# Eight products for V, Q and K in four of fifteen groups, and a new order on ScalarE and GpSimd

## The reference

```python
q = relu(h @ Wq + bq); k = relu(h @ Wk + bk); v = relu(h @ Wv + bv)   # h = layernorm(x)
e = q @ k.T / sqrt(512), causal: e - 10000 above the diagonal
y = softmax(e) @ v
x1 = x + layernorm(relu(y @ Wo + bo))
x2 = x1 + layernorm(ffn(layernorm(x1)))
```

## Time and profile before

| | us |
|---|---|
| median of 2 runs | 2149.94 (2148.06 to 2151.82) |
| the profiled execution | 2151.1 |
| its span, first to last instruction | 2149.3 |
| TensorE busy in the span | 1989.5 |
| VectorE | 1674.9 |
| ScalarE | 1146.2 |
| GpSimd | 1258.6 |

### The profile page before, as it was taken

How to read it: one execution, slowest core, us unless ns; L and a number is a source line. 1 busy time by engine, 2 the same in 40 slices (tenths; PEclk the granted TensorE clock), 3 DMA queues, 4 the chain that set the end, 5 groups by cost and what they waited for, 6 DMA issues and landing times. The chain is left out here.

```text
span 2149.3 us, 35197 instructions
## 1 busy us (share of the span) xinstructions
PE 1989.5 (93%) x11039; PEld 1103.9 (51%) x11039; DVE 1674.9 (78%) x3468; ACT 1146.2 (53%) x2496; POOL 1258.6 (59%) x1421
## 2 busy tenths in 40 slices
PE   7889999978999998899998799999999999999997
PEld 3555655555565554656555455544444444444443
DVE  8568665677766567767666776668999999999999
ACT  5444443344443434434333443333788888888885
POOL 6264452454534254453334634232899999999997
PEclk9999999999999999999999999999999999999999
DMA  6777656576865566766546676354222222222321
GB/s 216 205 177 158 171 139 157 124 196 170 159 179 155 131 163 142 184 171 170 145 126 170 157 177 143 98 140 117 66 99 84 95 98 84 98 94 84 100 82 65
DMA packets 379438, 295.00 MB, mean 137 GB/s; under 512 B 267890, under 2 KB 296178, under 8 KB 379252
## 3 DMA queue, kind: packets, MB, share of 16 engines
q1 hardware_dynamic: 353908, 212.00, 38.2%
q10 hardware_dynamic: 25344, 80.75, 13.8%
HBM read 165.27 MB, written 64.23 MB: 107 GB/s over the span
## 5 line engine op out<-in xcount | busy, mean ns | idle before, releaser
L724 PE MATMUL psum<-v,pT 128*128 128x512 f16 x1632 | 371.3, 385 | 21.3 <-DMA pT<-rows 21.3
L724 PE MATMUL psum<-kT,qT 128*128 128x512 f16 (+3 forms) x1920 | 367.3, 349 | 3.0 <-DVE rows L1478 3.0
L744 PE MATMUL psum<-hT_early,ring 128*128 128x256 f16 x2160 | 253.0, 277 | 37.8 <-ACT part L1061 35.3
L724 PEld LDWEIGHTS psum<-kT,qT 128*128 128x128 f16 x1920 | 182.4, 99 | 181.9 <-DVE rows L1478 4.4
L724 PEld LDWEIGHTS psum<-v,pT 128*128 128x128 f16 x1632 | 161.3, 99 | 210.1 <-issue 36.1
L1415 DVE SCALAR_TENSOR_TENSOR part<-psum,part 128x512 f32<-128x512 f32 x180 | 123.7, 687 | 172.1 <-ACT part L1061 107.9
L744 PEld LDWEIGHTS psum<-hT_early,ring 128*128 128x128 f16 x2160 | 212.0, 99 | 78.8 <-ACT part L1061 40.5
L1806 DVE MAX8 c<-cut 128x8 f32<-128x512 f32 x384 | 244.7, 679 | 0.0
L1061 ACT ACTIVATE part<-psum,bqkv_s 128x256 f32<-128x256 f32 x360 | 147.3, 466 | 124.8 <-PE psum L744 124.6
L744 PE MATMUL psum<-hT_late,ring 128*128 128x256 f16 x1620 | 190.6, 277 | 20.9 <-ACT part L1061 20.8
L724 PE MATMUL psum<-w_o,vT 128*128 128x512 f16 x768 | 174.7, 383 | 16.0 <-DVE kT L1409 7.5
(11 more groups left out here) (198 smaller groups left out, 3820.3 us busy)
## 6 DMA issues: line engine op xcount, KB each, us to landing
ring<-wc_scratch ACTq DMA_DIRECT2D x132, 512.0 KB, 4.1
xg<-x SPq DMA_DIRECT2D x64, 256.0 KB, 5.6
xr<-x SPq DMA_DIRECT2D x64, 256.0 KB, 3.4
h_scratch<-hb SPq DMA_DIRECT2D x64, 256.0 KB, 3.4
h<-h_scratch SPq DMA_DIRECT2D x64, 256.0 KB, 2.7
x<-x_scratch SPq DMA_DIRECT2D x64, 256.0 KB, 3.0
x_scratch<-xr SPq DMA_DIRECT2D x62, 256.0 KB, 3.9
out<-zn SPq DMA_DIRECT2D x59, 256.0 KB, 2.0
```

Of the source, the lines that this page charges most:

```text
L724: mm = nc.tensor.matmul(outp, stat(a), mov(c), start=(n == 0 and k == 0), stop=(n == total - 1 and k == 2))
L744: mm = nc.tensor.matmul(P_BANKS[p][:, 256 * m:256 * (m + 1)], ring[:, p, a, c, P * m:P * (m + 1)], h[:, b, c, :], start=(first and m + c + ...
```

## The change

**In the openings (1, 5, 9, 13)** V, Q and K are made with the ordinary eight block products, as four outputs of 24 matmuls that add up in a bank (`outputs`): output 0 in A and 1 in C in the first half step of a kind, 2 in B and 3 in A in the second. Output 3 waits for ScalarE's eviction of output 0; each output 0 for the eviction of the previous kind's output 3, and so does the first vo product, for K's. ScalarE evicts each output with four instructions of 256 columns, the float32 values to `part` and the float16 high half, both with ReLU from the bank (`output`); VectorE takes the low half by a subtraction (`lo_output`). There are no sums, no late quarters, no differences, and only half of the ring is used (two reloads a kind). ScalarE and VectorE have orders of their own for these halves.

**Elsewhere** the seven products stay. The ring's slots have a new order (`SLOTS`, `STORED`, `SLOT_OF`), so product 1 uses the third slot and waits for the second reload; refill(0) comes behind hi_11. In halves 2 and 4 copy_5 comes ahead of the exponential. On GpSimd, difference 7 moves from the end of half 5 to half 6, behind the two scales, and the late quarters from the end of half 6 to half 7, behind that half's two scales, both ahead of `residual`. Eight blocks of weights are stored for each kind (48 transfers in group 0), and the first ring load is two transfers instead of four.

```diff
 def stages(H):
...
     if g and kind != "vo":
-        return [("products", kind, g, h % 2)]
+        return [("outputs" if opening(g) else "products", kind, g, h % 2)]
...
+                def outputs(kind, g, i):
+
+                    def output(bank, t):
+                        for m in range(2):
+                            for j in range(2):
+                                for c in range(2):
+                                    for n, (a, b) in enumerate(((0, 0), (0, 1), (1, 0))):
+                                        mm = nc.tensor.matmul(bank[:, 256 * m:256 * (m + 1)], ring[:, 2 * i + j, a, c, P * m:P * (m + 1)],
+                                                              hT_early[:, g % 2, 2 * j + t, b, c, :], start=(m + j + c + n == 0),
+                                                              stop=(j + c == 2 and n == 2), skip_group_check=True)
+                        mm.then_inc(vqk_ps.sem, 1)
+
+                    pe.wait_ge(w_in[i], fetched(kind, g, i))
+                    if i == 0:
...
+                        vacated(kind, g, 0)
+                        output(A_BANK, 0)
+                        vacated(kind, g, 1)
+                        output(C_BANK, 1)
+                    else:
+                        vacated(kind, g, 2)
+                        output(B_BANK, 0)
+                        pe.wait_ge(vqk_ev.sem, vqk_ev.at(step_at(kind, g, 0)))
+                        output(A_BANK, 1)
...
+                def output(kind, g, o):
+
+                    i, t = divmod(o, 2)
+                    bank = (A_BANK, C_BANK, B_BANK, A_BANK)[o]
+                    act.wait_ge(vqk_ps.sem, vqk_ps.at(product_at(kind, g, o)))
+                    act.wait_ge(vqk_lo.sem, vqk_lo.at(lo_done(*ahead_of(kind, g), o)))
+                    for m in range(2):
+                        bias = bqkv_s[:, "qkv".index(kind), 2 * i + m:2 * i + m + 1]
+                        src = bank[:, 256 * m:256 * (m + 1)]
+                        nc.scalar.activation(part[:, o, 256 * m:256 * (m + 1)], src, ACT.Relu, bias=bias, scale=QKV_DOWN)
+                        a = nc.scalar.activation(placed(kind, g, i, t)[:, 0, m, :], src, ACT.Relu, bias=bias, scale=QKV_DOWN)
+                    a.then_inc(vqk_ev.sem, 1)
...
+                    elif kind and opening(g):
+                        if h in (2, 4):
+                            exponential(s)
+                        if h == 1:
+                            s = s_tile(H - 1)
+                        for o, span in ((2 * (h % 2), first), (2 * (h % 2) + 1, rest_of)):
+                            output(kind, g, o)
+                            if h in (1, 2, 4):
+                                hi_p(s, span)
+                        for n in ((1,) if h % 2 else (0, 2, 3)):
+                            refill(kind, g, n)
+                        if h == 0:
+                            exponential(s)
...
                     elif h in (2, 4):
                         if kind:
                             copy_1(kind, g)
+                            copy_5(kind, g)
                         exponential(s)
-                        if kind:
-                            copy_5(kind, g)
-                            refill(kind, g, 0)
                         hi_p(s, first)
                         if kind:
                             hi_11(kind, g)
+                            refill(kind, g, 0)
                             copy_u2(kind, g)
...
+                    elif h == 0 and kind and opening(g):
+                        lo_output(kind, g, 0)
+                        late(H, (2, residual_stats))
+                        lo_output(kind, g, 1)
+                        score_rows(s)
+                        late(H, (3, convolution))
+                    elif h == 1 and kind and opening(g):
+                        for o, span in ((2, first), (3, rest_of)):
+                            lo_output(kind, g, o)
+                            lo_p(s_tile(H - 1), span)
+                        late(H, (3, convolution))
+                    elif h in (2, 4) and kind and opening(g):
+                        score_rows(s)
+                        lo_output(kind, g, 0)
+                        late(H, (0, bias_o), (1, attention_stats))
+                        lo_p(s, first)
+                        lo_output(kind, g, 1)
+                        lo_p(s, rest_of)
+                        late(H, (2, residual_stats))
+                    elif h in (3, 5) and kind and opening(g):
+                        late(H, (3, convolution), (1, attention_stats), (2, residual_stats))
+                        lo_output(kind, g, 2)
+                        late(H, (0, bias_o))
+                        lo_output(kind, g, 3)
...
                         second_scale(due(H, 2))
+                    if h == 6 and g + 1 < NG and not opening(g + 1):
+                        difference(g + 1, 7, (1, 0), (0, 0), (1, 0))
+                    if h == 7 and g + 1 < NG and not opening(g + 1):
+                        for q in (4, 5, 6):
+                            lo_h(g + 1, q)
                     if due(H, 1) is not None:
                         residual(due(H, 1))
...
-                        difference(g + 1, 7, (1, 0), (0, 0), (1, 0))
-                    if h == 6 and g + 1 < NG:
-                        for q in (4, 5, 6):
-                            lo_h(g + 1, q)
```

More of the change, by code:

```diff
@@ L88, in run_of, with opening, events_ahead, lo_done @@
     return len(VQK) * (g - 1) + VQK.index(kind)
+def opening(g):
+    return 0 < g <= NG and GROUP * (g - 1) % TILES == 0
+def events_ahead(kind, g, whole, split):
+    runs = [(n, u) for u in range(1, g + 1) for n in VQK if (u, VQK.index(n)) < (g, VQK.index(kind))]
+    return FIRST + sum(whole if opening(u) else split for n, u in runs)
 def product_at(kind, g, p):
-    return FIRST + QUARTERS * run_of(kind, g) + p if g else plain_at(kind, C - 1)
+    return events_ahead(kind, g, 4, QUARTERS) + p
 def step_at(kind, g, e):
-    return FIRST + 8 * run_of(kind, g) + e if g else plain_at(kind, C - 1)
+    return events_ahead(kind, g, 4, 8) + e
+def lo_done(kind, g, n):
+    if g == 0:
+        return plain_at(kind, C - 1)
+    return step_at(kind, g, n if opening(g) else (LO_11, LO_12, LO_21, LO_22)[n])
+def last_lo(kind, g):
+    if g == 0:
+        return plain_at(kind, C - 1)
+    return step_at(kind, g, 3 if opening(g) else LO_21)
+def fetched(kind, g, n):
+    runs = [(m, u) for u in range(1, g + 1) for m in VQK if (u, VQK.index(m)) <= (g, VQK.index(kind))]
+    return 16 * (1 + sum(n < 2 or not opening(u) for m, u in runs))
+def split_groups(g):
+    return sum(not opening(u) for u in range(1, g + 1))
+def h_steps(g):
+    return sum(4 if opening(u) else 11 for u in range(1, g))
+def h_highs(g):
+    return sum(4 if opening(u) else QUARTERS for u in range(1, g))
 def ahead_of(kind, g):
@@ L858, in _ @@
                             products(*at)
+                        elif kind == "outputs":
+                            outputs(*at)
                         elif kind == "vo":
@@ L1676, in _ @@
                     elif h in (3, 5):
-                        if kind and opening(g):
-                            sum_12(kind, g)
-                            sum_22(kind, g)
                         late(H, (3, convolution), (1, attention_stats), (2, residual_stats))
-                        if kind and not opening(g):
+                        if kind:
                             sum_12(kind, g)
@@ L2002, in _ @@
                         mix(VQK[(H + 1) // 2])
-                    if h == 3 and g + 1 < NG:
+                    if opening(g + 1):
+                        if 3 <= h < 6:
+                            for q in ((0, 2), (1,), (3,))[h - 3]:
+                                lo_h(g + 1, q)
+                    elif h == 3 and g + 1 < NG:
                         lo_h(g + 1, 0)
```

134 lines of the change are left out of this document (75 added, 59 removed).

## The result

| | us |
|---|---|
| median before, 2 runs | 2149.94 |
| median after, 2 runs | 2120.87 (2120.62 to 2121.12) |
| ratio after to before | 0.9865 (95% interval 0.9822 to 0.9907) |
| span of the profiled execution | 2119.2, before 2149.3 |
| TensorE busy | 1991.3, before 1989.5 |

The change makes the kernel 29 us faster, 6 us short of the forecast 2115 and inside its range. The parts of the sum did not come out as forecast, though: one brought more, one brought nothing.

The account below looks back on a forecast made before the run. VectorE was taken as full in the second stage; in the first, TensorE's waits in and behind the openings could shrink. Gains 19.5 + 14 + 1.4 = 34.9 us off 2151.1 gave 2116, against median 2115; range 2090 to 2146.

Parts of the forecast that it names:

- Part 1: Eight products in openings 1, 5, 9, 13: 260.2 us together instead of 279.7, a gain of 19.5, ends 8 and 34.
- the pilot copy: Group 1: TensorE's existing 1.2-us wait for this copy was expected to stay.
- The work: TensorE's pure work per opening: 55.07 us plus 4.09 for 36 more matmuls, 59.2 us.
- The W_o wait: Openings: the first W_o product waits 1.9 us for the bank of K's last output, four copies and the hand-over.
- P of the last tile: Openings: TensorE waits for the last tile's P before its product, taken as 2.0 us, ends 0 and 6.
- the wait in Q: Groups 5, 9, 13: copy_5 wait goes; late score rows and exponential delay the Q outputs, reaching K about 1.2 us late.
- Part 2: GpSimd's scales first in half 7: 15.9 us of copy waits and 3 of clock go, net gain 14, ends -4 and 24.
- uncovered: 1 us: Group 0: 48 stores instead of 42 on SP's queue ahead of the ring's first load, counted as zero; 1 us if uncovered.
- the price of the late quarters: Groups 2, 6, 10, 11, 14: quarters behind second_scale delay hT_late and P transposes; 1 us each, 5 us, ends 0 and 20.
- rival D: Half 7 of all eleven seven-product groups: late hT_late delays product 4, 52 us lost against 35 gained, 2167; chance 0.05.
- Part 3: copy_5 ahead of the exponential in halves 2 and 4 of the other groups: gain 1.4 us, ends -3 and 4.
- Rival C: Shorter openings pack P and h transposes closer: 8 us given back there and 7 behind, 2136; chance 0.26.

Follow-up runs that it names:

- eight products alone: The changed kernel with GpSimd's order and ScalarE's copy_5 put back where they were, the openings' eight products kept: 2118.36 us, ratio 0.9859 to the kernel before.
- the run made for it: The changed kernel with group 1's last two transposes and the first ring load ahead of the stores of K's weights on SyncE's queue: 2115.76 us.
- the run with later reloads: The changed kernel with refill(0) and refill(1) of half 0 behind the exponential in the groups with seven products: 2096.29 us, ratio 0.9751 to the kernel before.

## Why the prediction was right, and where it was wrong

The total was close by luck: two errors of opposite sign nearly cancel. The eight products alone brought 29.3 us (2118.36 against 2147.66 beside it) where 19.5 was forecast, and the two other parts together nothing where 15.4 was.

- **Part 1, inside the openings: right.** 22.9 us against 19.5, 256.8 for the four against 260.2. Nearly all of the difference is group 1, 61.0 against 64.3, where neither a wait for P nor the one for the pilot copy was left; groups 5, 9 and 13 took 65.8, 66.5 and 63.4 against 65.3 each. The work was 59.4 to 59.7, put at 59.2. The W_o wait was 1.7 to 2.3, put at 1.9; P of the last tile 2.2, 1.2, 0 and 0, put at 2.0; the wait in Q showed as 2.1 to 2.3 us in front of output 3 where 1.2 in front of K was put. It comes from ScalarE standing before the exponential, which the walk had seen and not priced.
- **Part 1, around the openings: missed.** The sum ended at the opening's last matmul. The eight products alone also took 20.6 us out of the groups behind, because GpSimd and the P transposes come there sooner against TensorE (by the rows of group 6 and the waits given above). Part 2 had counted the copy waits there, 18.0 of its 20.8 us, as its own; half of them (9.0; 7.5 in the run with GpSimd's order back) went with part 1. In the run of the eight products alone groups 3 and 15 give 4.6 us each back, a wait of 2.8 for the copies with its clock. The prediction also gives its five copy waits as 3.11 to 5.78 us each; the shortest, in group 11, was 2.81, and the sum of 20.8 holds it rightly.
- **The start of group 1: missed.** The walk put "uncovered: 1 us" for the longer stores. TensorE waits 8.4 us there. It cost only 2.0 net, by luck: the relaxed wait ahead of group 0's first W_o product, which neither the description nor the prediction has, had made group 0 end 6.4 sooner. In the run made for it 9.0 came back at this place.
- **Part 2: the step that failed is the price of the late quarters**, "I take 1 us in each of five groups, 5 us; the ends are 0 and 20". Measured: 30.9 us of waits in eight groups, three of them groups for which nothing was taken, and the gain of 14 became nothing. The order of the queue was put right; the delay was not: in group 7, for which none was taken, the transposes went out 2.6 us ahead of the group's first matmul before, and go out 5.0 behind it now. That alone would have been carried, as the run with later reloads shows. What was missing is that refill(0) and refill(1) of half 0 go out at just that moment: the walk looked at what is ahead of the transposes on SP's queue, and not at what ScalarE's queue sends beside them. It had looked at that for P in the openings. The gross gain was priced too low as well: 24.5 us with the reloads out of the way, against 18.9 ahead of the price. The prediction's own sign for a wrong price, over 3 us for hT_late in groups 2, 6, 10 and 14, came true in all four (5.3, 3.7, 3.6, 7.5), and so did the one for rival D in groups 3 and 7 (2.7 and 5.0).
- **Part 3:** nothing, against 1.4.
- **Rival D** named the place (all groups with seven products, hT_late), and on the kernel before its mechanism alone made the time longer by 24 us. It was given 0.05. It did not decide here. The openings have no late quarters in the changed kernel, and on the kernel before three of them waited 8.1 to 9.4 us each; in the other groups the new waits came where the waits for the copies went. That this is the whole of the difference was not tested. Rival C, gains given back to transfers, has the right kind of cause and the wrong transfer.

## What to carry to other kernels

When a step is moved, list the transfers that every other queue issues in the same few microseconds, not only those ahead of it on its own queue: three transposes beside two 512-KB loads took 10.5 us instead of 2.8 to land, and it was enough to send the loads 7 us later, though they then flew beside the transposes of P, and the waits for P grew by 12 us. Two edits that each measure as nothing may be worth 24 us together, so a wait that vanished without a gain calls for a look at what took its place before the edit is dropped. An edit that shortens one stage also shifts the other engines against TensorE in the next one.

## What the runs showed of the hardware

- A group with one wait of TensorE of 2.8 us took 4.2 us more than without: behind the wait the granted clock was 0.50 for 2.74 us, then 1.00 again. Behind a wait of 2.3 us (Q's output 3 in group 5) 24 matmuls took 4.33 us at a mean granted clock of 0.62; behind the 1.76 us ahead of W_o it stayed at 1.00.
- The two kinds of transfer are not slowed alike: issued together in group 7 the two loads landed in 4.6 and 10.5 us (4.1 at the median before), the three transposes in 11.2, 10.5 and 8.0 (2.8). Whether this comes from their packets (4224 against 288 in that stretch) was not tried and stays open.
- The issue of a transpose stretches with it: SP's queue was held for 10.63 us by these three, and for 3.96 without the loads beside them, so what stands behind them on the queue is late too.
